# Who makes the middle bf16 part of x in an SSM front body: ScalarE or GpSimd

## The reference

```python
xr, gate = jnp.split(x @ W_in.T, 2, axis=-1)          # 512 channels each
xr = xr + t_emb[:, None, :]
xc = silu(causal_depthwise_conv4(xr, W_conv) + b_conv)
xn = (xc - mu) / jnp.sqrt(var + 1e-05) * ln_g + ln_b
Bm, Cm, dt = jnp.split(xn @ W_xproj.T, 3, axis=-1)    # 16 each
dt = jnp.tanh(dt @ W_dt.T + b_dt) * 0.01
Ad = 1.0 + dt * A
Bd = Bm * jnp.minimum(jnp.linalg.norm(xn, axis=-1, keepdims=True), 1.0)
# scan over 64 tokens
h = jnp.clip(h * ad[:, :, None] + bd[:, :, None] * xt[:, None, :], -10.0, 10.0)
yt = jnp.einsum('bd,bdh->bh', ct, h)
# after it
y = ys.transpose(1, 0, 2) + D * xn
x = x + y * silu(gate) @ W_out.T
```

## Time and profile before

| | us |
|---|---|
| median of 3 runs | 1788.49 (1788.26 to 1793.8) |
| span of the profiled execution | 1790.3 |
| TensorE busy | 1677.0 (94%) |
| VectorE busy | 1623.9 (91%) |
| ScalarE busy | 1307.1 (73%) |
| GpSimd busy | 686.9 (38%) |
| one front body (six in a loop in each layer) | 25.01 |

### The profile page before, as it was taken

How to read it: one execution, slowest core, us unless ns; L and a number is a source line. 1 busy time by engine, 2 the same in 40 slices (tenths; PEclk the granted TensorE clock), 3 DMA queues, 4 the chain that set the end, 5 groups by cost and what they waited for, 6 DMA issues and landing times. The chain is left out here.

```text
span 1790.3 us, 43798 instructions
## 1 busy us (share of the span) xinstructions
PE 1677.0 (94%) x14852; PEld 748.9 (42%) x14852; DVE 1623.9 (91%) x2492; ACT 1307.1 (73%) x2213; POOL 686.9 (38%) x702
## 2 busy tenths in 40 slices
PE   6999999999999999889999999999998899999998
PEld 3555555555554555332222224545553322222244
DVE  5899999999987999989999998679999899999975
ACT  5655556455546999889999993069998899999910
POOL 0223233232332332456666650012335576765500
PEclk9999999999999999899999999999998999999999
DMA  4000001000002344554545666624345445455678
GB/s 162 1 2 0 1 2 31 2 1 0 1 1 83 129 161 163 181 172 133 183 150 188 226 188 205 237 84 173 136 175 185 155 137 184 150 189 196 189 235 276
DMA packets 126456, 226.85 MB, mean 127 GB/s; under 512 B 35620, under 2 KB 61220, under 8 KB 117540
## 3 DMA queue, kind: packets, MB, share of 16 engines
q1 hardware_dynamic: 125912, 223.51, 37.9%
q10 hardware_dynamic: 432, 1.84, 0.3%
HBM read 141.95 MB, written 83.36 MB: 126 GB/s over the span
## 5 line engine op out<-in xcount | busy, mean ns | idle before, releaser
L1063 ACT ACTIVATE R<-q,Ast 128x512 f32<-128x512 f32 x1016 | 632.9, 708 | 34.5 <-DVE q L2085 32.3
L2085 DVE SCALAR_TENSOR_TENSOR q<-R,PS 128x512 f32<-128x512 f32 x1008 | 610.3, 677 | 9.6 <-ACT R L1063 5.9
L628 POOL TENSOR_TENSOR Uw<-Ub,rowmask 96x512 bf16<-96x512 bf16 x256 | 335.6, 1345 | 144.0 <-PE PS L1510 131.7
L1510 PE MATMUL PS<-xq,Uw 97*128 97x512 bf16 x1024 | 327.1, 391 | 46.5 <-DVE q L2085 37.8
L1527 PE MATMUL PS<-q,Wy 128*32 128x512 f32 x2016 | 279.8, 610 | 0.4 <-DVE q L2085 0.4
L1510 PEld LDWEIGHTS PS<-xq,Uw 97*128 97x128 bf16 x1024 | 84.9, 97 | 363.5 <-DVE q L2085 271.4
L1178 PE MATMUL PS<-X,Win 128*128 (+1 forms) x456 | 213.6, 606 | 0.1
L1079 PE MATMUL PS<-xn,Wl 128*128 128x512 f32 x384 | 186.6, 609 | 0.8 <-DVE xn L1649 0.7
L549 POOL TENSOR_TENSOR ex<-ex,rs 128x1024 f32<-128x1024 f32 x32 | 76.8, 2401 | 164.2 <-DVE rs L1672 164.2
L1767 DVE SCALAR_TENSOR_TENSOR acc<-xp,Wc,acc 128x512 f32<-128x512 f32 x192 | 134.5, 749 | 2.6 <-DVE eC L1889 0.2
L542 POOL TENSOR_TENSOR vsc<-vTd,vs_t 128x1024 f32<-128x1024 f32 x16 | 41.6, 2601 | 216.4 <-ACT vTd L773 216.4
(11 more groups left out here) (183 smaller groups left out, 2640.9 us busy)
## 6 DMA issues: line engine op xcount, KB each, us to landing
xq<-xpart_d SPq DMA_DIRECT2D x384, 192.0 KB
sg_d<-sg SPq DMA_DIRECT2D x16, 1024.0 KB, 5.3
xn_d<-z SPq DMA_DIRECT2D x16, 1024.0 KB, 3.9
y_d<-ys SPq DMA_DIRECT2D x64, 256.0 KB, 4.0
xnp<-xn_d SPq DMA_DIRECT2D x16, 1024.0 KB, 8.3
sgp<-sg_d SPq DMA_DIRECT2D x16, 1024.0 KB, 11.1
xpart_d<-xh SPq DMA_DIRECT2D x16, 512.0 KB, 2.9
xpart_d<-xmi SPq DMA_DIRECT2D x16, 512.0 KB, 3.7
```

The lines of the kernel that those rows point to most:

```text
L628: pl.tensor_tensor(Uw[0:XROWS, h, w, :, :, :], Ub[0:XROWS, w, 0:N, ds(s0, CH)].rearrange("p n t -> p t n").unsqueeze(2).broadcast_to([XROW ...
L1063: act.activation((end if end and (h, t) == (1, CH - 1) else R)[:, w, :], q[:, t % 2, w, :], ACT.Relu, scale=Ast[:, h, w, t:t + 1], bias=CL ...
L1510: pe.matmul(PS[:, w, :], Uw[0:KROWS, h, w, t, :, :].rearrange("p b n -> p (b n)"), xq[0:KROWS, hb, w, s8 % XT, :], start=True, stop=True). ...
L2085: v.scalar_tensor_tensor(out=q[:, s8 % 2, w, :], in0=R[:, w, :], scalar=2 * CLIP, in1=PS[:, w, :], op0=ALU.min, op1=ALU.subtract).then_inc ...
```

## The change

GpSimd makes the four casts of the rest to the middle part itself, each straight ahead of the subtraction that reads it, and waits for the rest (semaphore `xr1_r`) in place of ScalarE. ScalarE's `middle_part` and its four calls in each body are gone. This holds for the groups 0 to 6 of each layer; group 7 is as it was. In all 56 casts move.

```diff
@@ GpSimd, last_parts(it)
                     pl.wait_ge(eC_r, it + 1)
                     alone(pl)
                     for k in range(TT):
+                        pl.wait_ge(xr1_r, it * TT + k + 1 + TT)
+                        alone(pl)
+                        pl.tensor_copy(xmi[:, k, :], xr1[:, k, :]).then_inc(xmi_r, 1)
                         pl.wait_ge(xmi_r, it * TT + k + 1)
                         pl.tensor_tensor(xlo[:, k, :], xr1[:, k, :], xmi[:, k, :], ALU.subtract).then_inc(xlo_r, 1)
@@ ScalarE
-                def middle_part(it, k):
-                    act.wait_ge(xr1_r, it * TT + k + 1 + TT)
-                    act.activation(xmi[:, k, :], xr1[:, k, :], ACT.Copy).then_inc(xmi_r, 1)
@@ ScalarE, body(it, ahead)
                     if ahead:
                         tap(it + 2, 0)
-                    middle_part(it, 0)
-                    middle_part(it, 1)
-                    middle_part(it, 2)
-                    middle_part(it, 3)
                     square(it + 1, 0)
```

## The result

The change made the kernel slower. In the first comparison it took 1811.77 us (median of 4 runs, 1808.19 to 1818.87) against 1790.78 of before on the same chip: ratio 1.0112, 95% interval 1.0092 to 1.0132. A second comparison of the same two kernels later gave 1808.11 against 1791.12 us, ratio 1.0090 (1.0069 to 1.0111). By the ratios that is 20 and 16 us; the two intervals overlap. The prediction was 16.2 us more.

What follows compares the result with a forecast made beforehand. The prediction took the chain of VectorE and TensorE to bound the body. Twelve seams at 12.0 us plus 4.2 us for the seventh group make 16.2 us on the median of 1788.49: 1804.7 us, range 1794 to 1812.

Steps and rivals of the forecast that it cites:

- What bounds the body: SSM front body: the VectorE and TensorE chain bounds it; VectorE's root has no reserve, so its delay is not regained.
- Part 1: ScalarE's four casts in each of 14 bodies: 35 us busy time go, zero gain, since the squares wait for VectorE's centring.
- Part 2: GpSimd's work in a body: four cast and subtraction pairs take 7.24 us, ending at 644.75 and not 642.02; queueing costs nothing.
- Part 3: Seam between bodies: GpSimd's longer work holds up VectorE's SBUF-only cast, subtraction and root steps; 1.0 us a seam, 12.0 in all.
- Part 4: Seventh group's work in the scan: the four Uw behind it come late; 2.0 us a layer, 4.2 in all.
- Part 5: SP's store queue: stores wait for the last xlo, but ScalarE's high part has 2.1 us spare; cost zero.
- A: Seams: all hidden, GpSimd's fp32 subtraction does not keep VectorE out; 1789.3 us, no measurable change; chance 0.12.
- B: Squares in the body: ScalarE's queue is the bound there, so the kernel gets faster, 1756 us; chance 0.04.
- C: ScalarE's high part waits for slow store landings, some 1.0 us more in 12 bodies; 1816.7 us; chance 0.04.
- D: GpSimd's casts slower than 0.61 us or longer waits before subtractions: 0.5 more a seam, 1810.7 us; chance within forecast's 0.80.

## Why the prediction was right, point by point

**What bounds the body.** Right. VectorE's root had no reserve, and its delay went whole into the period: 1.03 us in a seam, 1.02 us of TensorE's waiting. I had read layer 0 only; layer 1's bodies were 25.11 us long before, and their seams cost 0.92.

**Part 1, ScalarE.** Right: no gain, and the wait ahead of the squares grew from 0.27 to 2.77 us. The busy time that went is 2.07 us a body and not 4 x 0.63, since consecutive activations overlap at their ends.

**Part 2, GpSimd's length.** Four pairs took 614.72 to 621.96, 7.24 us, the figure of the sum. They started 0.13 us later than put (637.63 in the old time), so they ended at 644.87, where the text has 644.75 and, worked through, 644.85.

**Part 3, the port.** One seam was put at 1.0 and measured 1.03. Step three was put at 645.32 and ended at 622.43 + 22.91 = 645.34. Within the seam the shares are other than I wrote: the cast ended a tenth later and the subtraction where it was put, root step one ended 0.26 sooner, as it took up the 0.19 us idle time ahead of it, and step two took longer, 1.00 us where I had listed 0.6 to 0.8. Only GpSimd's end counts for the sum, so this made no difference. Twelve seams: 12.0 us put, 12.2 (6.4 + 5.8) in the traces. They aren't equal: the last of each layer costs 1.26 us, which makes up for the smaller ones of layer 1.

**Part 4, the seventh group.** The distance from VectorE's first store copy to its second in the scan holds this place. Its values with ScalarE's casts, both layers: 12.65, 12.34 (before), 11.71, 12.35 (before, second trace), 12.34, 11.99 (loop's casts only). With GpSimd's: 14.30, 15.15 (changed), 13.28, 17.06 (changed, second trace), 15.45, 14.29 (seventh group only). The means are 12.2 and 14.9; the stretch behind gives 0.44 back (14.40 to 13.96). So 2.3 us a layer, where 2.1 was put. That the mean fits is in part luck, for it mixes two cases. In three of the six TensorE's granted clock was 1.00 throughout (14.30, 13.28, 14.29): there a join costs 1.3 us, less than put, though inside the ends of 0.4 and 2.65. In the other three (15.15, 17.06, 15.45) it fell to half for part of the distance, and a join costs 3.2. The sum has no term for the clock; the last section shows it.

**Part 5, the stores.** Right. SP's store of xlo went out at 623.45 + 22.91 = 646.36, put at 646.4, its median landing is 4.4 us, and ScalarE never waits for a DMA at the high part.

**Rivals.** A fell with the seam. B and C never appeared, nor did D: a cast takes 0.61 to 0.62 us and the subtraction starts 0.08 us behind it, as priced. The sum of 16.2 us stands against 16 and 20 us measured; it lies in the second interval and just under the lower end of the first (16.5 us). With the terms as measured it is 12.2 + 4.5 = 16.7 us. What the first comparison shows beyond that isn't explained by any change in the trace, and the second did not show it again.

## What to carry to other kernels

An engine that is three quarters idle isn't free, and semaphores aren't the only place where engines meet: before work is moved to GpSimd, look at which VectorE instructions will run beside it, and charge each that has two tensor inputs in SBUF, or copies from SBUF to SBUF, with the rest of the GpSimd instruction it meets. Instructions with an input in PSUM go beside it for nothing, so GpSimd's work belongs next to those, and a small intermediate that VectorE writes and reads again can be put in PSUM to get out of the way. That isn't quite free: it made the chain here 0.10 us longer. And relief for an engine is worth only what its next wait leaves: ask what its first instruction behind the removed work waits for.

## What was not expected of the hardware

VectorE gets in between two GpSimd casts, or between a cast and a subtraction (its own small cast took 0.57 and 0.53 us there, with GpSimd casts of 0.61 waiting behind), but not between memsets: there it took 1.79 us, through four of them. One kernel shows this, in its loop bodies; why it is so, no run tells.

TensorE's clock fell to half (1.2 GHz) behind the scan join of layer 1, and that is what sets the two cases of part 4 apart. TensorE had waited for Uw; in the second of these 4 us windows of the changed kernel its clock averages 0.57, and the same eight products take 1.57 us and not 1.07:

```profile
1404.00:1408.00 4.00, 2.33 (x44) 1.19 (x36) 3.13 (x6) 4.00 (x8) 4.00 (x6) 1.00 1.00 340
1408.00:1412.00 4.00, 4.00 (x46) 2.17 (x39) 0.79 (x3) 3.48 (x6) 4.00 (x4) 0.57 0.74 221
...
1407.52 0.39 PE L1505 MATMUL PS<-xq,Uw 97*128 97x512 bf16 x1 [0.90 <-POOL Uw L631]
1407.84 1.57 PE L1522 MATMUL PS<-q,Wy 128*32 128x512 f32 x8
...
1411.98 2.48 DVE L2080 SCALAR_TENSOR_TENSOR q<-R,PS 128x512 f32<-128x512 f32 x4 [3.21 <-PE PS L1505]
```

VectorE waits 3.21 us here where it waited 1.73 in layer 0 at full clock. So a short wait of TensorE can cost twice, once itself and once in the clock behind it. The same came in layer 1 of the second trace (one window at 0.50, eight products in 1.94 us, VectorE waiting 3.86) and in layer 0 of the kernel with the seventh group's casts alone. It doesn't come each time: in the other three joins with all four casts on GpSimd the same waits were not followed by a slower clock. But in the 20 joins of the other ten traces (one kernel among them with two casts a join) the clock was 1.00 over the same distance in each. So the slower clock comes with the moved casts; that TensorE's wait for Uw is what brings it down is likely, not shown.
